# Another order of the same steps: new urgencies in a planner, and transfers planned to wait for each other

## The reference

```
xn  = norm(norm(x)) * gamma + beta
dt  = softplus(xn @ W_dt.T + b_dt);  B = xn @ W_B.T;  C = xn @ W_C.T        # 16 states
h_t = exp(dt_t * A) * h_(t-1) + dt_t * B_t * xn_t;   y_t = sum_n C_t[n] * h_t[n] + D * norm(x)_t
x   = x + norm(y)
p   = softmax(norm(x) @ gate_w + gate_b);  the 2 best of 8 experts per token
x   = x + norm(sum over the 2 of p_e * (relu(norm(x) @ w1_e + b1_e) @ w2_e + b2_e))      # 128 -> 512 -> 128
```

## Time and profile before

| | |
|---|---|
| median of 3 runs | 473.23 us (472.01 to 474.21) |
| profiled execution, span | 473.8 us |
| PE busy | 413.7 us (87%), 2856 instructions |
| DVE busy | 350.2 us (74%) |
| ACT busy | 316.3 us (67%) |
| POOL busy | 294.6 us (62%) |
| moved by DMA | 125.5 MB, mean 265 GB/s |

### The profile page before, as it was taken

One profiled execution on the slowest core, in us unless ns is written; L12 is line 12 of the kernel. 1 busy time (PEld: TensorE's weight loads), 2 busy tenths in 40 slices (PEclk: granted clock), 3 DMA queues, 4 the chain that ended last, 5 costly groups with the idle time before them and its releaser, 6 DMA issues.

```text
span 473.8 us, 9865 instructions
## 1 busy us (share of the span) xinstructions
PE 413.7 (87%) x2856; PEld 323.4 (68%) x2878; DVE 350.2 (74%) x839; ACT 316.3 (67%) x826; POOL 294.6 (62%) x218
## 2 busy tenths in 40 slices
PE   7099999998899998989999994899899998999940
PEld 2056575464455557877887784899899997999830
DVE  5999899999999999979999998394333632002465
ACT  3857584762486586678998775585766776766833
POOL 1058366553989955279996369388676770777720
PEclk9579999999999999999999998899999998999965
DMA  7899988993999978999898999964887787866251
GB/s 190 285 386 338 367 295 319 289 311 141 271 350 334 384 234 297 316 304 370 313 415 326 335 302 188 408 218 115 250 219 224 204 227 215 217 183 182 74 156 44
DMA packets 78147, 125.50 MB, mean 265 GB/s; under 512 B 7832, under 2 KB 50592, under 8 KB 74000
## 3 DMA queue, kind: packets, MB, share of 16 engines
q1 hardware_dynamic: 73056, 116.00, 75.2%
q0 software_dynamic: 4320, 8.86, 5.9%
q10 hardware_dynamic: 720, 0.01, 0.1%
HBM read 105.95 MB, written 18.89 MB: 264 GB/s over the span
## 4 chain that ended last, share of the span: by engine, by line
PE 33%; DVE 10%; issue 6%; DMA 5%; ACT 5%; SPq 5%; ACTq 0%; DVEq 0%
PE out_ps L1292 12%; PE hid_ps L1280 7%; PE u_ps L1280 4%; DMA w_tile<-w_rows 3%; DVE u_ps L932 3%; PE y_ps L1196 2%; ACT hid_t L853 2%; PE misc L1250 2%; DMA xt<-slots_in 2%; DVE hs L941 2%; PE gx_ps L1280 2%; SPq L606 2%; SPq L586 2%; ACT mix L872 1%; PE misc L1242 1%
## 5 line engine op out<-in xcount | busy, mean ns | idle before, releaser
L671 POOL TENSOR_TENSOR ch<-hs,c_rep 128x1024 f32<-128x1024 f32 x64 | 151.0, 2362 | 84.4 <-DVE hs L941 54.3
L941 DVE TENSOR_TENSOR_SCAN hs<-ab,u_ps 128x512 f32<-128x512 f32 x128 | 150.6, 1204 | 0.2
L805 ACT ACTIVATE ab<-dt,decay 128x512 f32<-128x512 f32 x128 | 89.1, 719 | 44.3 <-DVE hs L941 43.3
L1292 PE MATMUL out_ps<-w_f,hid_t 128*128 x736 | 102.1, 282 | 4.7 <-ACT hid_t L853 2.8
L1292 PEld LDWEIGHTS out_ps<-w_f,hid_t 128*128 128x128 f32 x736 | 90.8, 194 | 11.0 <-issue 9.3
L853 ACT ACTIVATE hid_t<-hid_ps,w_tile 128x128 f32<-128x128 f32 x244 | 69.2, 377 | 30.3 <-PE hid_ps L1280 22.2
L1256 PE MATMUL y_ps<-none 128*128 128x512 bf16 x357 | 86.3, 380 | 1.0 <-issue 0.2
L932 DVE TENSOR_TENSOR u_ps<-b_rep,gx_ps 128x512 f32<-128x512 f32 x128 | 81.9, 679 | 1.0 <-DMA b_rep<-rows_dram 1.0
L689 POOL DMA_INDIRECT slots_in<-x,pos x64 | 64.2, 1003 | 27.4 <-issue 12.5
L1280 PE MATMUL hid_ps<-xt_t,w_tile 128*128 128x128 f32 x488 | 66.4, 281 | 9.4 <-DMA w_tile<-w_rows 8.5
L1196 PE MATMUL y_ps<-ident,ch 128*128 128x128 f32 x512 | 67.9, 277 | 5.5 <-POOL ch L671 4.5
(11 more groups left out here) (140 smaller groups left out, 467.8 us busy)
## 6 DMA issues: line engine op xcount, KB each, us to landing
b_rep<-rows_dram SPq DMA_DIRECT2D x64, 512.0 KB, 7.5
c_rep<-rows_dram SPq DMA_DIRECT2D x32, 1024.0 KB, 7.7
w_tile<-w_rows SPq DMA_DIRECT2D x92, 258.0 KB, 3.8
slots_in<-zeros SPq DMA_DIRECT2D x3, 1472.0 KB, 11.5
slots_out<-ot SPq DMA_DIRECT2D x33, 128.0 KB
xt<-slots_in SPq DMA_DIRECT2D x15, 256.0 KB
x<-x SPq DMA_DIRECT2D x8, 256.0 KB, 5.3
out<-mix SPq DMA_DIRECT2D x8, 256.0 KB, 2.7
```

The source lines that it names most:

```text
L671: nc.gpsimd.tensor_tensor(ch[:, n % NCH], hs[:, n % NH], c_rep[:, r // 2, 2 * (r % 2):2 * (r % 2) + 2].rearrange("p n t -> p (n t)"), ALU. ...
L805: nc.scalar.activation(ab[:, i % NA], dt[:, b % 2], ACT.Exp, scale=decay[:, 2 * r + h:2 * r + h + 1]).then_inc(s["decayed"], 1)
L941: nc.vector.tensor_tensor_scan(hs[:, n % NH, h * T:(h + 1) * T], ab[:, i % NA], u_ps[i % NU][:], 0.0, ALU.mult, ALU.add).then_inc(s["scann ...
L1292: last = nc.tensor.matmul(out_ps[:, j * D:(j + 1) * D], hid_t[:, q % NHT, c * P:(c + 1) * P], w2_f[:, bass.ds(e * HC * D + c * D, D)], sta ...
```

## The change

Every step's urgency moves from the calls of `at` into one table `URGENCY`, with other numbers for nearly every kind. `LANDING` becomes one constant of 2.4 us, and a table `MOVES` gives each kind of transfer a time by its size. In `planned` these times no longer run side by side: a transfer starts to move when the one issued before it is through. `COST` of `tile_weights` goes from 0.6 to 0.7. No step is added or taken away, and what a step does and waits for is untouched; the steps come in another order, the `warm` matmuls are 460 instead of 442, and `alone` is 35 instead of 41. All line numbers below the tables are 18 higher.

```diff
-    "weights_2": 0.4, "clear": 0.4, "rows_out": 0.4, "b_spread": 0.4, "tile_weights": 0.6, "tile_load": 0.4, "tile_store": 0.4,
+    "weights_2": 0.4, "clear": 0.4, "rows_out": 0.4, "b_spread": 0.4, "tile_weights": 0.7, "tile_load": 0.4, "tile_store": 0.4,
...
-LANDING = {"weights_2": 15.0, "clear": 16.0, "rows_out": 2.0, "spread": 5.5, "b_spread": 4.0, "tile_weights": 3.5, "tile_load": 2.8,
...
+LANDING = 2.4
+MOVES = {"weights_2": 7.2, "clear": 9.0, "rows_out": 0.15, "spread": 2.65, "b_spread": 1.4, "tile_weights": 0.85, "tile_load": 1.0,
+         "store": 0.5, "scatter": 0.3, "gather": 0.3, "tile_store": 0.5, "tile_send": 0.3, "yg_load": 1.0}
...
+URGENCY = {
+    "weights_2": 13, "clear": 25.5, "stats": 27.5, "scales_all": 20, "shift_all": 19, "norm": 14.5, "norm_first": 14.5,
...
-    def at(urgency, kind, i, part, *after):
-        todo[kind, i, part] = (urgency, [a for a in after if a in todo or a[1] >= 0])
+    def at(kind, i, part, *after):
+        todo[kind, i, part] = (URGENCY[kind], [a for a in after if a in todo or a[1] >= 0])
...
-        open_(key, free[engine] + LANDING.get(key[0], HOP))
+        if key[0] in MOVES:
+            moves_free = max(moves_free, free[engine]) + MOVES[key[0]]
+            open_(key, moves_free + LANDING)
+        else:
+            open_(key, free[engine] + HOP)
```

More of the change, by code:

```diff
@@ L100 @@
 }
-LANDING = {"weights_2": 15.0, "clear": 16.0, "rows_out": 2.0, "spread": 5.5, "b_spread": 4.0, "tile_weights": 3.5, "tile_load": 2.8,
-           "tile_store": 2.8, "store": 2.5, "scatter": 2.4, "gather": 2.4,
-           "tile_send": 2.4, "yg_load": 3.0}
+LANDING = 2.4
+MOVES = {"weights_2": 7.2, "clear": 9.0, "rows_out": 0.15, "spread": 2.65, "b_spread": 1.4, "tile_weights": 0.85, "tile_load": 1.0,
+         "store": 0.5, "scatter": 0.3, "gather": 0.3, "tile_store": 0.5, "tile_send": 0.3, "yg_load": 1.0}
 HOP = 0.18
+URGENCY = {
+    "weights_2": 13, "clear": 25.5, "stats": 27.5, "scales_all": 20, "shift_all": 19, "norm": 14.5, "norm_first": 14.5,
+    "turn": 24, "channels": 15, "states": 6.5, "rows": 24, "rows_out": 15.5, "delta": 13.5, "delta_first": 27,
+    "softplus": 29, "gx": 15, "norm_u": 4, "turn_u": 23, "skip_copy": 1, "spread": 29.5, "b_spread": 14, "drive": 37.5,
+    "decay": 4, "scan": 22, "weigh": 11, "reduce": 6, "y_stats": 21, "y_scale": 16.5, "x1": 3.5, "x1_scale": 7.5,
+    "x1_shift": 22.5, "x2": 18.5, "gate_turn": 14.5, "gate_copy": 7, "gate_logits": 25, "gate_bias": 13.5,
+    "gate_max": 30, "gate_exp": 24.5, "softmax": 19.5, "second": 2, "count": 15.5, "starts": 15, "slots": 12,
+    "scatter": 5.5, "id_shift": 12, "tile_ids": 2.5, "tile_load": 22, "tile_turn": 25, "tile_copy": 14,
+    "tile_weights": 0.5, "tile_pick": 9, "tile_up": 32.5, "tile_relu": 40.5, "tile_down": 18.5, "tile_keep": 11,
+    "tile_send": 7.5, "tile_store": 23.5, "weigh_turn": 22, "weigh_copy": 27.5, "yg_load": 8, "gather": 14.5,
+    "bias_mix": 22, "mix": 28.5, "mix_scale": 13.5, "mix_shift": 13, "result": 31, "add": 4, "store": 12.5, "dt_add": 7,
+    "dt_first": 2.5,
+}
 WARM, WARM_UP, HEAD_WARM, TURN_WARM = 0.26, 16.0, 14, 2
@@ L146, in tasks @@
         if b:
-            at(0, "norm", b, 0, ("shift_all", 0, 0), due)
+            at("norm", b, 0, ("shift_all", 0, 0), due)
         else:
[L149 to L154, removed]
+            at("norm_first", 0, 0)
@@ new lines, in tasks @@
+            at("reduce", n, 0, ("weigh", n, 0), ("skip_copy", b, 0), ("x1", b - 1, 0))
+        at("y_stats", b, 0, ("reduce", n0 + PAIRS - 1, 0))
+        at("y_scale", b, 0, ("y_stats", b, 0))
+        at("x1", b, 0, ("y_scale", b, 0))
+        at("x1_scale", b, 0, ("x1", b, 0))
+        at("x1_shift", b, 0, ("x1_scale", b, 0))
+        at("x2", b, 0, ("x1_shift", b, 0), *(("scatter", b - NX2, r) for r in range(TOPK * K)))
+        at("gate_turn", b, 0, ("x2", b, 0))
+        at("gate_copy", b, 0, ("gate_turn", b, 0))
@@ L235, in tasks @@
                *([("yg_load", b, 0)] if g == SENT else (("gather", b, r) for r in range(TOPK * K))))
[L236 to L241 removed]
+            at("mix", b, 0, ("bias_mix", b, 0), ("slots", len(GROUPS) - 1, 0))
```

120 lines of the change are left out of this document (58 added, 62 removed).

## The result

The changed kernel takes 476.98 us (median of 5, 476.26 to 478.17) where the kernel before takes 473.23 in the same session. The ratio is 1.0073 (95% interval 1.0044 to 1.0102): slower by 0.7%, where I had forecast 1.1% faster. The profiled execution has a span of 476.4 us, 2.6 more than that of before. It was the slowest of the five (478.17), so where a reading hangs on one or two us, the traces of later kernels with the same order of tiles and scans (e1, e6, e8) are put beside it.

What follows compares the result with a forecast made beforehand. DVE was taken to set the pace up to the last scan, then PE's tiles, then a mostly idle tail. Span 473.8 - 10.0 + 6.0 - 1.3 = 468.5 us, 467.9 as median, said as 468.0; range 461.5 to 476.5.

Steps and rivals of the forecast that it cites:

- the time is three lengths in a row: Whole kernel: 326.5 us to the last scan, paced by DVE, then 123.3 of tiles on PE, then 24.0 of tail.
- A: Rival: PE waits for weights queued behind a clearing, ACT behind PE, DVE behind ACT; 476.4 us, chance 0.16.
- B: Rival: DMA engines bound the scan part, so the last scan ends at 320.1 us; time 471.6 us, chance 0.16.
- D: Rival: DVE steps moved beside POOL's weigh turn out badly, by 5 us; time 473 us, chance 0.10.
- C: Rival: the order frees DVE wholly, last scan near 312 us; time 462 to 463 us, chance 0.10.
- Part 1: Up to 180 us: steps change places, DVE's work is the same; 0 us, bounds -1 and +2.
- Part 2: From 180 us to the last scan: DVE waits less with unchanged work; -10.0 us, last scan at about 316.5.
- the term on port meetings: Small DVE steps slowed beside POOL's weigh by a shared SBUF read interface: 0 us, bounds -5 and +6.
- The 8.4 us for the clearing: Before the last scan: moving the last clearing removes DVE's 7.3 and 1.1 us waits on ACT for sequence 6; -8.4 us.
- Part 3: Tiles after the last scan: more tile halves on PE, two stalls fewer, one new wait; +6.0 us, bounds +2 and +12.
- Both stalls on `xt`: After the last scan: PE's waits for first token loads of group 2 and the last group should go; -5.7 us.
- Part 4: The tail: mix of sequence 5 begins 1.1 to 1.6 us behind the last tile; -1.3 us, bounds -3 and +1.

Runs made afterwards that it cites:

- e1: The changed kernel without the 57 filler matmuls behind the first tile_up: 476.6 us, 1.0099 of the kernel before.
- e6: The changed kernel with the clearings of groups 2 and 3 each cut into four transfers: 479.7 us, 1.0142 of the kernel before.
- e8: The changed kernel with the last clearing moved back behind tile 31's weights, where the old order had it: 477.8 us, 1.0091 of the kernel before.
- e11: The changed kernel with three extra DVE memsets (3.3 us) ahead of the drives of pair 62: 478.5 us, 1.0111 of the kernel before.
- e7: The kernel before with only the last clearing moved, ahead of tile 26's weights instead of tile 32's: 474.8 us, 1.0049 of the kernel before.
- e5: The kernel before with the clearings of groups 2 and 3 each cut into four transfers: 469.9 us, 0.9906 of the kernel before.
- e9: The changed kernel with tile_relu 9, 10, 19, 20 put ahead on ACT and tile halves replacing 32 fillers: 479.4 us, 1.0125 of the kernel before.
- e13: The changed kernel with split clearings and four tile halves with their relus ahead of sequence 6's gate_turn: 479.3 us, 1.0116 of the kernel before.
- e14: e13 together with the relus put ahead as in e9: 478.3 us, 1.0114 of the kernel before.
- e17: The changed kernel with sequence 6's x1_shift ahead of pair 56's scans and its x2 ahead of two decays: 476.3 us, 1.0035 of the kernel before.
- e18: The changed kernel with 12 fillers (some 2.7 us of PE) ahead of the reduce of pair 59: 479.6 us, 1.0103 of the kernel before.
- e16: The kernel before with split clearings, tile_relu 14, 15, 21 put ahead on ACT, and the three tile halves of e15: 469.3 us, 0.9928 of the kernel before.
- e15: The kernel before with split clearings and three tile halves put ahead of the reduce of pair 54: 469.3 us, 0.9926 of the kernel before.
- e2: The kernel before without its 37 fillers behind the first tile_up: 473.7 us, 1.0028 of the kernel before.

## Why the prediction was wrong

**The picture.** The failed step is the first one: "the time is three lengths in a row", with the last scan as the joint. In the kernel before PE and DVE meet within 0.3 us at that joint, so it looked as if all behind it waited for DVE. But PE does not wait there in the kernel before either: it works through from 300.87 to 338.71 without a wait of 0.2 us or more and only happens to have no backlog. In the new order it has 4.2 us of it, and DVE's gain stops counting at that point. Set against the sum, the span is 7.9 us longer than forecast: the last scan 2.3 us late, PE 3.9 us late behind it, 2.0 more from tile 35 to the last tile (131.0 us, forecast 129.0), and a tail 0.3 shorter. So the joint is the largest piece and not the only one.

None of the signs that I had named for being wrong came up. The last scan ended before 321, and no new wait on transfers of over 4 us stands in the tile part. Of the rivals, A has almost the measured time (476.4), which is luck: it needed DVE's wait for the root back and the last scan at about 325, and neither is there. For B, the transfers, the DMA share up to the last scan is 0.95 and the scan ended at 318.8, between the forecast's 316.5 and B's 320.1; its time, 471.6, is built on the same joint as the forecast's. D has half of its 5 us (DVE's busy time grew by 2.6), and C's last scan near 312 did not come.

**Part 1** held: 0 forecast, the first `tile_up` came 0.4 us earlier.

**Part 2** held in its waits and missed in its work. DVE's idle time up to the last scan fell from 25.2 to 14.9 us, -10.3 where I had said -10.0, and the only named wait left is 3.6 us on the logits. But DVE's busy time there grew from 301.3 to 303.9. This is the term on port meetings, which I had set to 0 within -5 and +6. The two groups that make most of it, to be held against the earlier trace rows (count, busy us, mean ns):

```profile
L1002 DVE TENSOR_TENSOR r_sub<-logit,r_max 128x64 f32<-128x64 f32 x4 | 6.4, 1600 | 0.1
L1047 DVE TENSOR_TENSOR_SCAN run<-restart,tot 128x64 f32<-128x64 f32 x4 | 5.2, 1296 | 0.1
```

`r_sub` was 4.8 and `run` 2.6: +4.2 us together, partly made good elsewhere. In e1, with the same DVE order, the busy time up to the last scan is 302.6, so part of the growth belongs to this one execution. It counts little in the time of the changed kernel: up to some 2 us are taken up by DVE's reserve (e11).

**The 8.4 us for the clearing** were the right reading of that wait and the wrong price. e7 shows the step by itself at no gain, and e8 no difference that can be told for its place in the new order. I had named rival A as a thing that happens or doesn't, with all of the 8.4 us or none. In three of these four kernels PE stood still for a load behind the last clearing (6.7 us before, 2.6 changed, 7.5 in e7), in e8 it did not, and only the split in the old order (e5) lowered the time. The remark that no load came late but those behind the clearing is wrong as well: the two loads of tokens that PE waited for at 338.71 and 394.54 have no clearing ahead of them.

**Part 3** is where the time went. Forecast +6.0, measured 123.3 to 135.2, +11.9. Of this 3.9 is the backlog at the joint (4.2 instead of 0.3), the step that failed, and 8.0 are the tiles from tile 35 on. The wait of `reduce` 63 for `weigh` (+1.7) did not come, because PE was late for it. The work (+9.4) was about right: from tile 35 on PE is busy for 8.8 us more. Both stalls on `xt` went as said, but I had taken off 5.7 us for them and the time lost behind the last scan fell only from 5.6 to 4.8: new small waits came, two on `ot` with 1.7 us together and more between the halves.

**Part 4** held: `mix` of sequence 5 begins at 455.20, 1.2 us behind the last tile, and the tail is 1.7 us shorter (forecast 1.3).

**Span and time.** I took 0.6 us off because the span before stood above the median. Every execution since lies 1.7 to 2.2 us above its own span (478.17 for 476.4). So the profiled execution before was some 2.4 us above its median (473.8 + 1.8 against 473.2), which says nothing of the next kernel. The one after lies 1.2 us above its own. The change of the span alone, +2.6, is within the interval of the ratio, and the medians differ by 3.8.

**What stays open.** Why PE had 8.8 us less tile work ahead of its meeting. The lumps on ACT are visible and e9 shows that opening two of them does not help by itself; e13 and e14 were to show that it helps together with tiles ahead of the meeting, and did not. Nor was it tested whether the transfers hold the tiles back there: between the first `tile_up` and the meeting the DMA share is 0.96 before and 0.99 in the changed kernel. That the time goes by the meeting and the work behind it rests on the difference of e17 and e18 (3.3 us of an expected 4 to 5.5); e13 to e16, which were to show it by way of the tiles, did not. The best version is the old order with the clearings split, e5 or e15: 469.9 and 469.3 us, 0.7 to 0.9% faster than the kernel before.

## What to carry to other kernels

When two engines take turns as the bound, don't cut the time where one ends. Follow the chain of waits back from the end to the last long wait of the late engine for another; the time is that moment plus the work that its stream holds behind it. The work can be counted from the order before anything runs (here 8 halves and 2 turns more, 8.0 us), the moment can't, and clock and small waits moved the stretch by 1 to 2 us from one execution to the next. An order that fills the early engine's gaps and moves work of the late one behind that point can lose. Read the early engine's reserve too: at each of its last results, how long before use it is ready (here 2.1 us at pair 62, with POOL's queue between). A stall on one queue can move with each reordering and still cost the same: before trusting a better place for the transfer, move it alone (e7), and try it in smaller pieces (e5 gained 3.2 us, e6 none).

## What the runs showed of the hardware

- Fillers on PE paid for themselves and no more: without 57 of them the time lost fell by 7.5 us and PE's own work grew by 6.9 (e1), without 37 by 4.4 and 3.3 (e2).
- SP itself stands still at the transfer behind a large one: 6.0 us for a 258 KB load behind 1.48 MB before, 8.56 in the changed kernel, 2.74 in e8, where the whole clearing is issued at 299.24, and 2.0 in e6 for the load behind a piece of 0.39 MB (that piece itself once took 3.8 us to issue).
- Small DVE operations beside a `weigh` on POOL: the four `run` scans took 0.65 us each on average before and 1.30 in the changed kernel, with the same shapes. In both traces each `run` and `r_sub` that meets a `weigh` ends within 0.2 us of that `weigh`'s end (0.48 to 2.42 us), and each that meets none takes 0.22 to 0.29 us. The Trainium skill ("SBUF — State Buffer", section "Who interferes with whom") says that a DVE instruction with two SBUF inputs contends with a GpSimd instruction that reads SBUF, and that the second to issue is blocked until the first finishes; the traces agree.
